# Writing out the loop over the middle batches in a gated linear attention and mixture-of-experts kernel

## The reference

```python
q = l2norm((x @ Wq).reshape(B, T, H, DK));  k = l2norm((x @ Wk).reshape(B, T, H, DK))
v = (x @ Wv).reshape(B, T, H, DV);          alpha = sigmoid(x @ Wg).reshape(B, T, H, DK)
def step(S, qkva):                       # over the T tokens, for each batch and head
    S = a_t[..., None] * S + k_t[..., None] * v_t[:, :, None, :]
    return S, einsum('bhkv,bhk->bhv', S, q_t)
x = layernorm(x + o.reshape(B, T, H * DV) @ Wo)
h = moe(swiglu(x @ lin0_w + lin0_b));    h = swiglu(h @ lin1_w + lin1_b)
out = layernorm(x + h)
```

## Time and profile before

| | us |
|---|---|
| time, median of 3 runs | 2013.74 (2011.88 to 2014.73) |
| the profiled execution | 2015.12 |
| its span, first to last instruction | 2013.3 |
| PE busy | 1769.1 (88%), 29575 matmuls |
| DVE busy | 1595.3 (79%) |
| ACT busy | 1194.5 (59%) |
| POOL busy | 936.1 (46%) |
| mean granted clock of PE | 0.960 of 2.4 GHz |

### The profile page before, as it was taken

How to read it: one execution, slowest core, us unless ns; L and a number is a source line. 1 busy time by engine, 2 the same in 40 slices (tenths; PEclk the granted TensorE clock), 3 DMA queues, 4 the chain that set the end, 5 groups by cost and what they waited for, 6 DMA issues and landing times.

```text
span 2013.3 us, 75320 instructions
## 1 busy us (share of the span) xinstructions
PE 1769.1 (88%) x29575; PEld 1411.6 (70%) x29575; DVE 1595.3 (79%) x3391; ACT 1194.5 (59%) x2608; POOL 936.1 (46%) x731
## 2 busy tenths in 40 slices
PE   6998888898888888888988888899879999999997
PEld 5777767777777777677777777677756666666664
DVE  6898779797878787797978787788957778787775
ACT  6766656565656566565656565566635555555553
POOL 6554445454545444454545454445514444444443
PEclk9999989899999999899999999999989999999998
DMA  7000000000000000000000000000000000000000
GB/s 195 8 3 9 3 8 3 8 2 8 8 3 8 3 8 3 8 3 8 2 8 8 3 8 3 8 3 8 3 12 11 11 21 21 10 21 10 21 16 11
DMA packets 28580, 26.13 MB, mean 13 GB/s; under 512 B 1928, under 2 KB 23696, under 8 KB 28304
## 3 DMA queue, kind: packets, MB, share of 16 engines
q1 hardware_dynamic: 28304, 21.77, 3.7%
HBM read 13.38 MB, written 4.19 MB: 9 GB/s over the span
## 4 chain that ended last, share of the span: by engine, by line
PE 42%; issue 22%; DVE 18%; POOL 11%; ACT 5%; DVEq 1%; POOLq 0%; DMA 0%; ACTq 0%; SPq 0%
DVE k_sb L1236 6%; PE bank L674 5%; PE bank L532 5%; PE bank L622 5%; POOL wq_lo L500 4%; POOL wk_lo L500 4%; PE bank L533 4%; PE bank L534 4%; PE bank L664 4%; PE bank L581 3%; PE bank L619 3%; DVE s_sb L1274 3%; PE bank L638 3%; DVE tot_sb L320 2%; PE bank L607 2%
## 5 line engine op out<-in xcount | busy, mean ns | idle before, releaser
L456 POOL TENSOR_TENSOR sq_lo<-sq_sb,sq_hi 128x512 bf16<-128x512 f32 x256 | 330.2, 1290 | 533.3 <-ACT sq_hi L962 532.1
L1236 DVE TENSOR_TENSOR qq_sb<-qq_sb,tot_sb 128x512 f32<-128x512 f32 (+1 forms) x384 | 257.7, 671 | 177.3 <-PE bank L619 173.6
L1236 DVE TENSOR_TENSOR k_sb<-k_sb,tot_sb 128x512 f32<-128x512 f32 (+1 forms) x384 | 379.3, 988 | 3.5 <-PE bank L622 2.2
L461 POOL TENSOR_TENSOR rn_sb<-ss_sb,expo 128x8 f32<-128x8 f32 x128 | 214.8, 1678 | 122.3 <-DVE ss_sb L1281 122.3
L1009 ACT ACTIVATE at_sb<-diag_sb 32x256 f32<-32x256 f32 x256 | 106.0, 414 | 202.7 <-DVE diag_sb L1248 198.0
L984 ACT ACTIVATE v_sb<-bank,rn_sb 128x128 f32<-128x128 f32 x512 | 139.0, 383 | 71.3 <-PE bank L534 68.1
L500 POOL TENSOR_TENSOR wq_lo<-v_sb,wq_hi 128x512 fp32r<-128x512 f32 x80 | 103.7, 1296 | 146.8 <-ACT wq_hi L1132 146.8
L500 POOL TENSOR_TENSOR wk_lo<-v_sb,wk_hi 128x512 fp32r<-128x512 f32 x80 | 104.2, 1302 | 134.0 <-ACT wk_hi L1132 134.0
L619 PEld LDWEIGHTS bank<-qq_sb,k_sb 128*32 128x32 f32 x12288 | 123.9, 110 | 58.7 <-issue 40.9
L664 PE MATMUL bank<-v_sb,at_sb 128*128 128x128 f32 x1024 | 147.5, 287 | 18.2 <-DVE res L1288 18.2
L619 PE MATMUL bank<-qq_sb,k_sb 128*32 128x16 f32 x12288 | 141.6, 185 | 20.8 <-DVE k_sb L1236 12.1
(11 more groups left out here) (204 smaller groups left out, 4820.7 us busy)
## 6 DMA issues: line engine op xcount, KB each, us to landing
x_nat<-in_L_attn_x_dram SPq DMA_DIRECT2D x16, 256.0 KB, 3.8
x_nat<-x_all SPq DMA_DIRECT2D x16, 256.0 KB, 2.4
out_dram<-k_sb SPq DMA_DIRECT2D x16, 256.0 KB, 2.3
ew_raw<-in_L_ffn_exp_w_dram SPq DMA_DIRECT2D x3, 512.0 KB, 5.8
qq_sb<-in_L_attn_Wq_dram SPq DMA_DIRECT2D x1, 512.0 KB, 3.9
qq_sb<-in_L_attn_Wk_dram SPq DMA_DIRECT2D x1, 512.0 KB, 5.9
k_sb<-in_L_attn_Wg_dram SPq DMA_DIRECT2D x1, 512.0 KB, 6.7
k_sb<-in_L_attn_Wv_dram SPq DMA_DIRECT2D x1, 512.0 KB
```

The lines of the kernel that those rows point to most:

```text
L456: nc.gpsimd.tensor_tensor(sq_lo[:, n, :], sq_sb[:, n % 2, :], sq_hi[:, n, :], ALU.subtract).then_inc(sq_done, 1)
L461: nc.gpsimd.tensor_tensor(rn_sb[par][:, i, :, :].rearrange("p h c -> p (h c)"), ss_sb[:, i * G:(i + 1) * G], expo[:, 0:G], ALU.pow).then_i ...
L1236: return nc.vector.tensor_tensor(view, view, by, ALU.mult)
```

## The change

On the four compute engines the hardware loop becomes a Python loop, so that the body stands fourteen times in each engine's stream, each time with its own constants. Nothing else is touched: SP and the feed-forward stage keep their loops, and the tiles, buffers, semaphores and the order of the real work stay.

```diff
@@ POOL @@
-            with pool.Fori(1, B - 1) as b:
+            for b in range(1, B - 1):
                 body(b)
@@ PE @@
-            with pe.Fori(1, B - 1) as b:
+            for b in range(1, B - 1):
                 body(b)
@@ ACT @@
-            with act.Fori(1, B - 1) as b:
+            for b in range(1, B - 1):
                 body(b)
@@ DVE @@
-            with dve.Fori(1, B - 1) as b:
+            for b in range(1, B - 1):
                 body(b)
```

## The result

The changed kernel takes 1908.55 us (median of 4 runs, 1905.75 to 1911.58) against 2013.26 before: a ratio of 0.948, 95% interval 0.9461 to 0.9499. The forecast was 1913, within 1896 to 1934. The profiled execution took 1910.43 us.

A forecast was written before the change was run, and what follows sets the result against it. Bound: a chain of waits between PE and DVE, with PE's jump back stalling each looped batch. Jumps 87.6 us, constants 5.6 and fewer clock falls made a gain of 100 us: 1913 us, range 1896 to 1934.

The forecast's parts named there:

- The sum: Batches 1 to 14: 84.5 us each, 1183 us in place of 1283.0, a gain of 100 us.
- The jump on PE: First slots of batches 2 to 14: removing 13 jumps back gives 6.74 us each, 87.6 us.
- The half clock behind the stall: First slot after each jump: PE busy 5.85 us at clock 0.50; up to 2.9 us lost, 2.57 by the slot.
- The later clock fall: Last two slots of a batch: 1.01 us, not tied to the jump, taken to fall in half of the batches.
- The far end with two falls in every batch: Batches 1 to 14: two falls each and nothing from constants, 86.4 us a batch, gain 73, time 1941.
- The jumps of DVE, ACT and POOL: Loop ends of these engines: 45 to 67 ns a jump, at most 0.9 us in all, taken as 0.
- Constants for registers: Register waits in 14 batches become constants: 0.4 us a batch, 5.6 us; bounds 0 and 17 us.
- Longer streams to fetch: DVE, ACT and POOL fetch about 5 packets in each of 13 more batches: taken as 0, far end 21 us lost.
- One of the prediction's own signs of being wrong: DVE in the changed kernel: the prediction is wrong if DVE shows idle time put down to issue.
- The other signs named in advance: No L788 branch, no PE issue idle over 1 us at batch start, first slots 19.5 to 19.9 us, clock about 0.98.
- the locked clock: Rival: the clock falls in two slots of every batch, 86.0 us each, gain 79, time 1935; chance 0.12.
- The stall of the short engines: Rival: DVE, ACT and POOL stall on fetches, 3.46 us a packet, 17 us a batch, time 2140; chance 0.02.

The follow-up runs named there:

- the repeated execution: The changed kernel run once more with nothing altered, on the same chip as the run with the feed-forward loops written out: 1910.15 us (1903.5 to 1910.34).

## Why the prediction was right

- **The sum.** The forecast gain of 100 us was 87.6 for the jumps, 5.6 for the constants and the rest, some 7, for fewer clock falls. Measured from the slot marks of the two traces, 105.2 us are 86.3, about 10.8 and about 8. The mechanism and the largest term were right; the constants were too small by half.
- **The jump on PE.** Forecast 13 x 6.74 = 87.6 us, with 6.74 read from batch 2 alone. Over all thirteen batches the first slots were 6.64 us longer than that of batch 1, together 86.3. The first slots of the fourteen batches give back 364.2 - 275.3 = 88.9; the 2.6 beyond the jumps are constants. That the cause is PE's jump back, and not the loop or the other engines, is shown three times: PE alone carries 100 us; six jumps in place of thirteen give half; one jump leaves one long slot. That it is dear because the code has left the engine rests on the other runs: a PE body short enough to stay has no excess, a medium one has, and the short engines stall as soon as their bodies are doubled. The instruction packets of the kernel before show the fetch itself. In the first jump, whose branch lasts from 196.32 to 199.65 us, PE's instruction queue moved one packet from 197 to 198.5 us, none up to 200, and one from 200 to 201.5:

```profile
q8 instruction: 1, 0.02, 3.9%
q8 instruction: 1, 0.02, 5.3%
```

  At all thirteen jumps a packet starts 0.9 to 1.5 us after the start of the branch, the branch ends 1.4 to 1.5 us after the packet has landed, and a second packet starts 0.6 to 0.9 us after that end. The second idle stretch ends 1.3 to 1.6 us after the second packet has landed, again at all thirteen.
- **The half clock behind the stall.** Forecast as part of the 6.74. In the kernel after, a clean batch ran at 1.00 through its first slot and the stretch of 5.85 us at 0.50 has no successor. How the 6.74 split into stall and clock was read from the trace and not separated by a run.
- **The later clock fall.** Forecast in half of the batches, 7 falls in fourteen. The profiled execution had 7. That this was exact is luck: the repeated execution had 2, and its fourteen batches took 5.0 us less, 1 us a fall. Three of the 7 came in the second slot, which the rows before had never shown. The far end with two falls in every batch was given as a loss of 14.1 us; by its own numbers it is 15.2, since batch 1 would gain two. The time of 1941 was worked out another way and does not change. The spread of the changed kernel's eight runs, 1903.5 to 1911.6 us with clocks from 0.992 down to 0.985, is put down mostly to this; only two of the eight have a trace.
- **The jumps of DVE, ACT and POOL.** Forecast 0; the first slot of the run with only PE written out (19.50 us) is not longer than without them (19.60).
- **Constants for registers.** Forecast 0.4 us a batch against batch 1 of the kernel before. A clean batch after is 280.72 - 197.10 = 83.62 us, 0.76 under the 84.38. This term was too small by half, some 5 us in all, and is the largest part of why 1908.55 came in under 1913. I had read it from the first two slots of batch 15 and given the others 0.05 each. The last two have more. One mark of the kernel before parts them, the start of slot 4 of batch 1:

```profile
173.66 0.68 DVE L1208 TENSOR_TENSOR e_sb<-qq_sb,k_sb 128x512 f32<-128x512 f32 x1
```

  Batch 1 before and batch 2 after take 19.85 and 19.60 us in slot 1, 21.98 and 21.94 in slot 2, 20.75 and 20.64 in slot 3, 21.80 and 21.44 in slot 4: 0.25, 0.04, 0.11 and 0.36 less. Batch 15 could not show the last two, because a clock fall lay over the one and the other has different work.
- **Longer streams to fetch.** Forecast 0. One of the prediction's own signs of being wrong did come by the letter: DVE's waits in the fourteen batches of the changed kernel have a line put down to issue that the kernel before lacks,

```profile
DVE qq_sb L1236 <- issue: 6.2, 18, 0.6
```

  Fourteen of the 18 stand in the first slots, mostly 0.22 us before one certain instruction. In batch 1 of the kernel before, the same instruction waited as long, put down to PE:

```profile
125.14 1.55 DVE L1236 TENSOR_TENSOR qq_sb<-qq_sb,tot_sb 128x512 f32<-128x512 f32 x1 [0.20 <-PE bank L619]
```

  So most of it is an old wait under another name. That none of the 18 is a late instruction is not shown; but the first slots, at 19.6 to 19.8 us, leave no room for more than 0.3 us. The packets were 44 more on the short engines' queue, not 65, and 30 fewer on PE's, not 26: without register instructions the bodies are shorter (PE's batch has 3511 instead of 3599 instructions by the trace, DVE's 203 instead of 279).
- **The other signs named in advance.** No branch, no idle time of PE over 0.6 us put down to issue, first slots of 19.6 to 19.8 us, a clock of 0.986 for "about 0.98": as said. A batch "in 83.6 to 85.4" held for seven of the fourteen; the three with two falls took 85.5 to 86.0, and four clean ones 83.2 to 83.5.

Of the rivals, the locked clock did not come in the changed kernel, but nearly did in the run with two loops of seven, where the clock fell in most batches. The stall of the short engines is real, but needs a jump: in these runs straight code came in time but for the 0.1 to 0.3 us a batch left open above, and a jump to a long body did not.

## What to carry to other kernels

When a written-by-hand loop has a long body, look at the branch's own line and at the first instructions behind it on each engine, and compare the pass that is entered from above with those entered by the jump: that difference is the whole price, read without any model. Look at the granted clock of that first pass too: in the run with all but PE written out, batch 1 had two clock falls and took 86.1 us, and the same comparison would have given 5.1 us a jump, where the kernel before gave 7.8. If the body can't be made short enough to stay with its engine, write the loop out, first on the engine that the others wait for; on an engine with slack a dear jump may be hidden, and a mean over the loop says nothing about it. Count a stall of PE with the slow clock that follows it, here 2.6 us on top of 4.2.

## What the runs showed of the hardware that was not expected

A jump to code that is gone shows on PE in the duration of the branch (3.3 to 3.9 us), on DVE and ACT only in the time until the next sequencer instruction (2.9 us behind a branch of 63 ns on DVE, 2.6 us behind one of 45 ns on ACT); whoever reads only branch durations misses it there. On PE there is a second stall of 1.64 us a little later, in the middle of a group of equal matmuls, and it came 118 instructions after the jump: the next packet was not on its way while the branch waited. With half as many matmuls in that group it did not come, and the jump cost 4.1 us instead of 6.6. And register instructions of 40 ns (76 more a batch on DVE alone), mostly in the shadow of other work, still came to some 0.3 us a batch of 84 on three engines.
